# Key projections of a cross-attention: the fifth matmul of a block contracts 128 rows instead of 64

## The reference, cut to what matters

```python
qh = _split_heads(jnp.einsum('bnq,qi->bni', x, Wq))
kh = _split_heads(jnp.einsum('bmc,ci->bmi', context, Wk))    # this product
vh = _split_heads(jnp.einsum('bmc,ci->bmi', context, Wv))
sim = jnp.einsum('hid,hjd->hij', qh, kh) * SCALE
mean = jnp.mean(sim, axis=-1, keepdims=True)
sim = (sim - mean) * ATTN_MATRIX_SCALE + mean
attn = jax.nn.softmax(sim, axis=-1)
out = jnp.einsum('hij,hjd->hid', attn, vh)
```

## Time and profile before

| | |
|---|---|
| median of 3 runs | 2608.7 us (2606.54 to 2611.08) |
| span of the profiled execution, first to last instruction | 2603.9 us |
| TensorE matmul busy | 2543.7 us, 98% |
| TensorE weight load busy (overlaps matmul) | 2283.5 us, 88% |
| VectorE busy | 1914.2 us, 74% |
| ScalarE busy | 1606.5 us, 62% |
| GpSimd busy | 158.2 us, 6% |

### The profile page before, as it was taken

The page is one execution under the profiler, slowest core; times in us unless marked ns, Lnnn a source line. Parts: engine busy times, 40 slices in busy tenths (PEclk is TensorE's granted clock), DMA queues, the critical chain, the costliest instruction groups (busy, mean ns, idle before and its releaser), DMA issues. The chain is left out here.

```text
span 2603.9 us, 47026 instructions
## 1 busy us (share of the span) xinstructions
PE 2543.7 (98%) x17647; PEld 2283.5 (88%) x17647; DVE 1914.2 (74%) x3606; ACT 1606.5 (62%) x3049; POOL 158.2 (6%) x208
## 2 busy tenths in 40 slices
PE   8999989999999999999999999999999999999998
PEld 6899868998899889988999899988998899889987
DVE  5888767776777677767777777767776777677787
ACT  6899646555666555565566466656665566556566
POOL 1344220000000000000000000000000000000003
PEclk9999999999999999999999999999999999999999
DMA  8765350001100120011000300020001200110001
GB/s 246 211 162 147 101 221 25 17 17 65 66 17 25 57 74 17 16 66 65 25 16 15 116 17 16 17 108 31 17 17 57 74 17 16 65 68 17 28 1 33
DMA packets 60638, 155.47 MB, mean 60 GB/s; under 512 B 8849, under 2 KB 22353, under 8 KB 60465
## 3 DMA queue, kind: packets, MB, share of 16 engines
q1 hardware_dynamic: 56464, 140.15, 16.7%
q0 software_dynamic: 3248, 12.72, 1.6%
q10 hardware_dynamic: 752, 0.26, 0.0%
HBM read 125.70 MB, written 27.39 MB: 59 GB/s over the span
## 5 line engine op out<-in xcount | busy, mean ns | idle before, releaser
L1731 ACT CAST pt_hi<-xt_ps 128x512 fp32r<-128x512 f32 x1024 | 592.4, 585 | 568.9 <-PE xt_ps L1698 553.0
L1810 DVE TENSOR_TENSOR pt_lo<-xt_ps,pt_hi 128x512 fp32r<-128x512 f32 x1024 | 704.4, 688 | 255.4 <-ACT pt_hi L1731 252.1
L1799 DVE TENSOR_SCALAR_CACHE_REDUCE xprobs<-xs_ps 128x1024 f32<-128x1024 f32 x512 | 626.6, 1224 | 176.1 <-PE xs_ps L1638 171.4
L1709 PE MATMUL xo_ps<-pt_hi,v_hi 128*128 128x256 f32 x2048 | 647.3, 316 | 2.4 <-DVE pt_lo L1810 2.3
L1737 ACT ACTIVATE xprobs<-xprobs,xneg_max 128x1024 f32<-128x1024 f32 x512 | 591.4, 1155 | 27.2 <-DVE xneg_max L1805 27.2
L1698 PE MATMUL xt_ps<-ident,xprobs 128*128 128x128 f32 x4096 | 603.7, 272 | 0.0
L1709 PE MATMUL xo_ps<-pt_hi,v_lo 128*128 128x256 f32 x2048 | 571.3, 279 | 0.0
L1709 PE MATMUL xo_ps<-pt_lo,v_hi 128*128 128x256 f32 x2048 | 570.0, 278 | 0.0
L1698 PEld LDWEIGHTS xt_ps<-ident,xprobs 128*128 128x128 f32 x4096 | 484.1, 140 | 61.9 <-issue 6.7
L1709 PEld LDWEIGHTS xo_ps<-pt_hi,v_hi 128*128 128x128 f32 x2048 | 386.3, 189 | 5.7 <-DVE pt_lo L1810 2.6
L1709 PEld LDWEIGHTS xo_ps<-pt_lo,v_hi 128*128 128x128 f32 x2048 | 388.3, 190 | 2.0
(11 more groups left out here) (251 smaller groups left out, 2736.3 us busy)
## 6 DMA issues: line engine op xcount, KB each, us to landing
v_split<-ctx_split SPq DMA_DIRECT2D x68, 768.0 KB, 5.8
xq<-x_split SPq DMA_DIRECT2D x64, 512.0 KB, 3.2
q_st<-rel_split SPq DMA_DIRECT2D x32, 256.0 KB, 3.8
q_st<-q_split SPq DMA_DIRECT2D x32, 192.0 KB, 4.6
k_st<-k_split SPq DMA_DIRECT2D x32, 192.0 KB, 4.7
ctx_split<-ctx_out POOLq DMA_DIRECT2D x8, 768.0 KB, 4.1
q_split<-attn_late SPq DMA_DIRECT2D x8, 512.0 KB, 4.0
k_split<-attn_late SPq DMA_DIRECT2D x8, 512.0 KB, 5.5
```

Of the source, the lines that this page charges most:

```text
L1709: last = pe.matmul(o_ps[:, 0:GQ], v[:, vs], pt[:, c % 3, GQ * j:GQ * (j + 1)], start=c == 0 and j == 0 and m == 0, stop=c == PIECES - 1 an ...
L1731: act.copy(pt_hi[:, c % 3, :], t_ps[:, c % 3, :]).then_inc(t_rounded, 1)
L1799: dve.tensor_scalar(probs[:, par if kind == "A" else 1 - par, t, CHUNK * i:CHUNK * (i + 1)], s_ps[:, buf, :], LOGIT, None, ALU.mult, ALU.m ...
L1810: dve.tensor_tensor(pt_lo[:, c % 3, :], t_ps[:, c % 3, :], pt_hi[:, c % 3, :].bitcast(F32), ALU.subtract).then_inc(t_ready, 1)
```

## The change

The fifth matmul of a block takes all 128 rows of part 2 and of the tail weights' rests, where it took rows 0 to 63. It now makes lo by lo of the tail beside hi by lo. The other four matmuls are as before, and so are the number of instructions, their order, the loads and the waits. The number of rows is no longer listed, since it is 128 for all five.

```diff
-                passes = [(kv_split[:, 0, 0, :], 0, P), (kv_split[:, 0, 1, :], 0, P), (kv_split[:, 0, 0, :], 1, P),
-                          (kv_split[:, 1, 0, :], 2, P), (kv_split[0:TAIL, 1, 1, :], 2, TAIL)]
+                passes = [(kv_split[:, 0, 0, :], 0), (kv_split[:, 0, 1, :], 0), (kv_split[:, 0, 0, :], 1),
+                          (kv_split[:, 1, 0, :], 2), (kv_split[:, 1, 1, :], 2)]
                 for b in (2 * i, 2 * i + 1):
-                    for n, (weights, part, rows) in enumerate(passes):
-                        rows_of = ahead[b][0:rows, part, :] if ahead else blocks[0:rows, b % 4, part, :]
+                    for n, (weights, part) in enumerate(passes):
+                        rows_of = ahead[b][:, part, :] if ahead else blocks[:, b % 4, part, :]
                         last = pe.matmul(s_ps[:, buf, BLK * (b % 2):BLK * (b % 2 + 1)], weights, rows_of,
                                          start=n == 0, stop=n == len(passes) - 1)
```

## The result

The changed kernel took 2587.6 us in the median of 5 runs (2585.01 to 2588.65), the kernel before 2607.8 us beside it. The ratio is 0.9923, with a 95% interval of 0.9912 to 0.9933, so 20.2 us are gone. The forecast was 2588.1 us.

A forecast was written before the change was run, and what follows sets the result against it. PE was taken as the bound, its matmuls setting their own pace. 19.9 us from 28 chunks plus 0.7 us from BEFORE's last chunk made 20.6 us, 2608.7 to 2588.1 us, with a range of 2584 to 2594 us.

The forecast's parts named there:

- The holes: Key projections: each change between 128 and 64 rows leaves a hole in PE's matmuls; 0.71 us a chunk, bounds 0.56 to 0.76.
- rule that spoke against the change: Weight loads: 32 rows take the time of 128, only columns count; by this alone nothing is gained, 2608.7 us.
- first rival: Fifth matmul: the hole belongs to an accumulation's end and the next bank's start, not row count; 2608.7 us, chance 0.05.
- The size: Key chunks between pieces: 28 chunks in seven heads by 0.71 us give 19.9 us, bounds 15.7 and 21.3 us.
- The new fifth matmul: Fifth matmul at 128 rows: taken at 0.233 us; at 0.34 us the 58 blocks that count would give back 6.4 us.
- What hides what: Heads' key chunks: ScalarE and VectorE don't become longer than PE, and the blocks' next loads still land in time.
- the room ahead of `K+2`: Between the end of K+0 and K+2's window: 7.8 us, 7.1 us after the change, against loads landing in 5.8 us.
- BEFORE: Four early key chunks: three gains vanish into waits for loads, Q+ stays near 362 us; only K+3's 0.7 us counts.
- to take nothing for the clock: Q+ and K+3 in BEFORE: longer waits might lower the granted clock, costing nothing to 1.7 us; nothing was taken.
- The row of the same place before: Waits of 355 to 365 us in BEFORE: granted clock stayed at 1.00, so no cost was taken for a fall.
- a fall of the clock after 370 us: Anywhere after 370 us: a falling granted clock was named as one sign that the prediction is wrong.
- The sum: Whole kernel: 20.6 us less, span 2603.9 to 2583.3 us, median 2608.7 to 2588.1 us.

The follow-up runs named there:

- half: Kernel before, with only the first block of a chunk keeping its fifth matmul at 64 rows and the second taking 128: 2597.5 us, ratio 0.996.
- adjacent: Kernel before, with a chunk's second block taking its 64-row matmul first, so that the two 64-row matmuls stand side by side: 2596.5 us, ratio 0.9958.
- second: Kernel before, with the 64-row matmul moved from last to second place in its block: 2610.9 us, ratio 1.0017.
- after_again: The changed kernel measured once more, nothing altered: 2588.3 us, ratio 0.9929 to the kernel before.
- rows96: Kernel before, with the fifth matmul contracting 96 rows in place of 64: 2591.9 us, ratio 0.9934.
- warm: Changed kernel plus 7 and 12 unused matmuls in the waits ahead of BEFORE's third key chunk and first query projection: 2586.1 us, ratio 0.9928.
- warm_late: Like `warm`, with the last key chunk of a head one piece later: 2587.1 us, ratio 0.9925.

## Why the prediction was right, and where it was off

*The holes.* The mechanism was right, and shown in both directions. Idle time of the weight path ahead of the 64-row loads goes with the change of the row count: 21.9 us before, 10.9 us in `half`, 11.0 us in `adjacent`; it moves with the change in `second` and doesn't come with 96 rows. The Trainium skill gives a reason in TensorEngine Tiling (Array Packing), section Key Properties: "Changing tiling mode (not just tile) drains the TensorE". The trace agrees as far as it goes, though no run shows the mode itself: at either change the weights load only when their own matmul starts, while within 128 rows a load starts one matmul ahead, and 96 and 112 rows behave as 128. The Trainium skill's rule that spoke against the change (TensorE: Matmul & The Clock Gate, section LDWEIGHTS (loading the stationary operand)), that a load's row count doesn't matter, holds here for the load's duration (183 against 188 ns) and doesn't cover the pace around it. The 0.195 us that a change costs is about the length of one such load; that the load, no longer hidden, is the cost is likely but not shown.

Two details of the prediction's first rival were misread. The scores end two accumulations of three matmuls each, not three, and what lies ahead of the fifth matmul is 0.10 of the 0.39 us, not half. `second` settles that rival without them.

*The size.* 0.71 us a chunk was forecast. Six heads from first chunk to first chunk took 2249.98 - 603.23 = 1646.75 us before and 2234.28 - 604.02 = 1630.26 us after: 16.49 us for 24 chunks, 0.69 us each. Two of these heads lose time to loads (next paragraph). In the others a head takes 271.62 us against 274.47 us, 2.85 us less or 0.71 us a chunk, as forecast. The new fifth matmul costs the 0.233 us that was taken and not 0.34 us: ten starts in 2.33 us.

*What hides what.* ScalarE and VectorE cost nothing, as forecast: no wait for `pt_lo` or `k_lo` stands among PE's waits in the steps. The loads were mis-sized. I took 5.8 us from issue to landing, the median of all, and set it against the room ahead of `K+2`. It is `K+3` that comes short: the second load of its pair takes 7.7 to 8.4 us in the seven heads after, and 5.7 to 7.5 us before. `K+3` came 0.24, 0.14 and 0.35 us late in three heads, 0.7 us in all, and took 2.41 us in place of 2.33 us each time, so that these heads lost 1.0 us. PE's list has only one of these waits. The weight path's has all three under `k_lo` (0.8 us, in the line of 300 loads above), but `K+3` doesn't wait for that `k_lo`, the one of `K+2`, and its first load starts 0.10 to 0.11 us after the landing in each of them. The loss varies: in `after_again` and `rows96` `K+3` was up to 0.72 and 1.11 us late, 2.1 us in the seven heads of each.

*BEFORE.* That three chunks vanish into the waits for loads was right to 0.03 us at `Q+`. Its last chunk was to gain 0.7 us and lost 0.8 us. The step that failed was to take nothing for the clock; it took 1.5 us, as the added matmuls show, within the bound of 1.7 us. The row of the same place before, from which I took nothing, was no guide. But that the change brought the fall on, by its longer waits, is not shown. `second` waits 0.44 and 2.40 us there, less than the 0.67 and 2.59 us before, and its clock fell as well. Of nine profiled executions it fell at `Q+` in six: `after`, `after_again`, `half`, `adjacent`, `rows96` and `second`. It stayed up in `before`, `warm` and `warm_late`. So it may come to the kernel before too, and the 1.5 us are what it costs, not what the change costs.

The prediction also named a fall of the clock after 370 us as a sign against it. The trace after has none before 2584 us, where PE has done its work. `after_again` has one, 0.50 in 2545 to 2547 us, but so has `second`, which has all its holes, with a mean of 0.97 from 2500 to 2600 us. It doesn't bear on the holes.

*The sum.* The span was to be 2583.3 us and is 2585.8 us, 2.5 us more: 1.5 us for the clock and 1.0 us for the heads with late loads. That the median agrees within 0.5 us owes something to chance: 20.2 us are gone between the medians and 18.1 us between the two traces. The trace before came from an execution at the fast end of its runs, 2 to 3 us under the median if it also lay 1.8 us under its time, and the trace after from one at the median.

## What to carry to other kernels

Look for idle time at issue ahead of weight loads whose shape differs from their neighbours': here the 64-row matmul's own 183 ns told nothing, and the two changes of the array around it cost 0.39 us. Where data or zeros for the other rows are at hand, contract all 128; where they aren't, put the small matmuls side by side, which here was worth half of it (10.4 of 20 us). A shorter chunk ahead of a wait for a load gains nothing, and the granted clock behind such a wait is worth a look in more than one trace: its fall cost 1.5 us here and was missing from the one trace that the forecast was made on.

## What was not expected of the hardware

A change costs ahead of the matmul and again behind it, some 0.10 us each, so even a second 64-row matmul right behind the first starts 0.33 us after it and not 0.233 us. And 0.7 us less between two pairs of 768 KB loads (4.6 us in place of 5.3 us) made the later one's last load land after 7.7 to 8.4 us, where it took 5.7 to 7.5 us before. The trace before had the same to show elsewhere: the other two pairs of a head, issued 4.2 us apart, have their last load land after 7.6 to 9.2 us. Why so little less room costs so much isn't settled by these runs.
